# Attention's Strassen products on one Trainium2 core: two banks filled turn by turn in place of one after the other

## The reference

```python
memory_proj = jnp.einsum('bme,de->bmd', memory, W_mem)
scores = jnp.einsum('bnd,bmd->bnm', hidden_states, memory_proj) / jnp.sqrt(jnp.float32(D))
attn = jax.nn.softmax(scores, axis=-1)
memory_context = jnp.einsum('bnm,bmd->bnd', attn, memory_proj)
gate_input = jnp.concatenate([hidden_states, memory_context], axis=-1)
gate = jax.nn.sigmoid(jnp.einsum('bnf,df->bnd', gate_input, W_gate) + b_gate)
fused = hidden_states + gate * memory_context
return _rmsnorm(fused, norm_w)
```

## Time and profile before

| | us |
|---|---|
| median of 3 runs | 933.08 (931.79 to 933.41) |
| the profiled execution, its own time | 933.24 |
| its span in the trace | 931.5 |
| PE busy | 915.3 (98%), 4412 matmuls and 4412 weight loads |
| DVE busy | 738.0 (79%) |
| ACT busy | 415.3 (45%) |

### The profile page before, as it was taken

The page is one execution under the profiler, slowest core; times in us unless marked ns, Lnnn a source line. Parts: engine busy times, 40 slices in busy tenths (PEclk is TensorE's granted clock), DMA queues, the critical chain, the costliest instruction groups (busy, mean ns, idle before and its releaser), DMA issues.

```text
span 931.5 us, 11731 instructions
## 1 busy us (share of the span) xinstructions
PE 915.3 (98%) x4412; PEld 770.8 (83%) x4412; DVE 738.0 (79%) x969; ACT 415.3 (45%) x624; POOL 53.9 (6%) x74
## 2 busy tenths in 40 slices
PE   9999999999999999999999999999999999999996
PEld 8878888888888887788888888888888888888884
DVE  5975767776777669968786589888889888988887
ACT  5442222232222224554545456555555656555553
POOL 0000000000000000000000011001111111111002
PEclk9999999999999999999999999999999999999999
DMA  9433567546575646675648925555555544545542
GB/s 352 169 134 114 208 221 233 218 168 230 190 261 190 234 155 223 247 238 204 212 152 321 371 90 197 204 203 203 203 182 185 179 171 183 170 172 184 204 181 90
DMA packets 50408, 187.41 MB, mean 201 GB/s; under 512 B 5168, under 2 KB 7216, under 8 KB 43312
## 3 DMA queue, kind: packets, MB, share of 16 engines
q1 hardware_dynamic: 50064, 186.14, 56.2%
q10 hardware_dynamic: 288, 0.52, 0.2%
HBM read 130.02 MB, written 56.62 MB: 200 GB/s over the span
## 4 chain that ended last, share of the span: by engine, by line
PE 85%; DVE 7%; issue 4%; ACT 2%; DMA 1%; SPq 1%; POOL 0%; DVEq 0%; POOLq 0%; ACTq 0%
PE psum L1271 28%; PE psum L1273 28%; PE psum L1272 28%; DMA g_raw<-in_g 1%; DVE g_l L796 1%; ACT yh L536 1%; DVE yt_raw L949 1%; PE psum L1353 1%; DVE b_l L796 0%; DVE y L1006 0%; DVE wn_l L796 0%; DVE ws_l L796 0%; DVE z L907 0%; SPq L286 0%; DVE g_raw L824 0%
## 5 line engine op out<-in xcount | busy, mean ns | idle before, releaser
L1271 PE MATMUL psum<-g1h,xh 128*128 128x512 f32 x448 | 175.3, 391 | 2.3 <-DVE k_out L917 2.2
L1272 PE MATMUL psum<-g_l,xh 128*128 128x512 f32 x448 | 174.8, 390 | 0.0
L1271 PEld LDWEIGHTS psum<-g1h,xh 128*128 128x128 f32 x448 | 84.5, 189 | 21.0 <-issue 3.5
L1273 PE MATMUL psum<-g1h,xs_l 128*128 128x512 f32 x256 | 100.3, 392 | 0.0
L1272 PEld LDWEIGHTS psum<-g_l,xh 128*128 128x128 f32 x448 | 84.5, 189 | 17.5
L536 ACT ACTIVATE xh<-xs_raw 128x512 fp32r<-128x512 f32 x64 | 40.3, 632 | 121.6 <-PE psum L1273 121.6
L1172 DVE TENSOR_TENSOR zb<-psum,zb 128x512 f32<-128x512 f32 x112 | 76.8, 686 | 15.8 <-PE psum L1273 15.7
L907 DVE TENSOR_TENSOR z<-psum,bias 128x512 f32<-128x512 f32 x64 | 44.2, 690 | 39.7 <-PE psum L1273 39.7
L1273 PE MATMUL psum<-g1h,xsum_l 128*128 128x512 f32 x192 | 74.7, 389 | 0.0
L507 POOL TENSOR_TENSOR stat<-stat 128x1 f32<-128x1 f32 x30 | 19.7, 658 | 860.1 <-ACT zb L739 860.1
L536 ACT ACTIVATE xh<-xsum_raw 128x512 fp32r<-128x512 f32 x48 | 30.1, 629 | 80.8 <-PE psum L1273 75.8
(11 more groups left out here) (172 smaller groups left out, 2417.5 us busy)
## 6 DMA issues: line engine op xcount, KB each, us to landing
xs_raw<-in_xt SPq DMA_DIRECT2D x16, 1024.0 KB, 4.8
z_spill<-z SPq DMA_DIRECT2D x16, 1024.0 KB, 7.8
b_raw<-in_xt SPq DMA_DIRECT2D x32, 512.0 KB, 6.5
zb<-z_spill SPq DMA_DIRECT2D x16, 1024.0 KB, 6.9
xrow<-in_x SPq DMA_DIRECT2D x30, 512.0 KB, 6.6
out<-xrow SPq DMA_DIRECT2D x30, 512.0 KB, 3.7
y_spill<-y SPq DMA_DIRECT2D x32, 256.0 KB, 2.7
yt_raw<-y_spill SPq DMA_DIRECT2D x16, 512.0 KB, 3.6
```

The source lines that it names most:

```text
L1271: nc.tensor.matmul(tile, ah, mh, start=start, stop=False, skip_group_check=True)
L1272: nc.tensor.matmul(tile, ah, ml, start=False, stop=False, skip_group_check=True)
L1273: return nc.tensor.matmul(tile, al, mh, start=False, stop=stop, skip_group_check=True)
```

## The change

In `mem_gate` the waits for both halves are now issued ahead of all matmuls of a product, and then the 12 matmuls go mem, gate, mem, gate, with the same stationary slice for both of a pair: for each k (0, 1) and part (high-high, high-low, low-high) one matmul of mem and one of the gate. `mem_mm` is raised by the 11th matmul in place of the 6th, `gate_mm` by the 12th as before. Product 6 of batch 15 keeps the old form. So 111 of 112 products are changed. Number, shapes and operands of the matmuls are the same, and so is what each bank accumulates.

```diff
--- before.py
+++ after.py
@@ -1436,10 +1436,23 @@
                             pe.wait_ge(z_done, P7 * b)
                         elif i >= 2:
                             pe.wait_ge(z_done, P7 * b + {2: 1, 3: 2, 4: 3, 5: 4, 6: 5}[i])
+                    if final:
+                        for k in range(2):
+                            last = three(bank(bk), th[:, slot, k, :], tl[:, slot, k, :], wb_h[m][i][:, k, :],
+                                         wb_l[m][i][:, k, :], False, k == 1)
+                        last.then_inc((mem_mm, gate_mm)[m], 1)
+                if not final:
+
                     for k in range(2):
-                        last = three(bank(bk), th[:, slot, k, :], tl[:, slot, k, :], wb_h[m][i][:, k, :],
-                                     wb_l[m][i][:, k, :], k == 0 and i in (0, 1, 3), k == 1)
-                    last.then_inc((mem_mm, gate_mm)[m], 1)
+                        for part in range(3):
+                            for m in range(2):
+                                bk = 2 * m + (p if i in (0, 2, 4, 6) else 1 - p)
+                                last = nc.tensor.matmul(bank(bk), (tl if part == 2 else th)[:, slot, k, :],
+                                                        (wb_l if part == 1 else wb_h)[m][i][:, k, :],
+                                                        start=k == 0 and part == 0 and i in (0, 1, 3),
+                                                        stop=k == 1 and part == 2, skip_group_check=True)
+                                if k == 1 and part == 2:
+                                    last.then_inc((mem_mm, gate_mm)[m], 1)
```

## The result

| | before | changed |
|---|---|---|
| median of 12 runs, us | 933.04 (931.44 to 935.40) | 935.26 (933.66 to 936.33) |
| the profiled execution, its own time | 933.24 | 934.14 |
| its span | 931.5 | 932.4 |
| weight loads, matmuls | 4412, 4412 | 4412, 4412 |

The ratio is 1.0020, 95% interval 1.0011 to 1.0029: slower by 1.9 us (1.0 to 2.7), distinct from no difference, and right on the bound of 0.2% that the prediction set. The forecast was 935.0.

The account below looks back on a forecast made before the run. It took PE, busy 98% of the span, as the bound, with matmul rate unchanged. Rate 0, batch 1 0.2 and batch 15 1.74 sum to +1.9 us over the 933.08 median: 935.0, range 933.4 to 937.2.

Parts of the forecast that it names:

- bound of 0.2%: Whole kernel: a measurement can tell about 0.2% (1.9 us) from no change, 934.95; 50% slower, 45% same, 5% faster.
- Nothing idle on TensorE, rate unchanged: Attention's products: PE busy 25.33 of 25.33 us a batch; matmuls stay 0.227 us apart, sharing and alternating banks cost 0.
- price of 0.230 us a matmul: Upper bound on the rate: 0.230 us in place of 0.227 for 1332 matmuls would cost 4.4 us.
- Rival 3: Clock falls after batch 15's new 0.6 us stall: 1.7 us more, 936.7; chance 4%.
- Price of a late release: Attention's products: first matmul starts 0.15 us behind a late release, 0.08 more lost after; 0.23 ahead costs nothing.
- Batch 1, +0.2: Product 2 of batch 1 waits for z_out, starting 557.30 instead of 557.18, then loses 0.08 more: +0.2 us.
- Batch 15, product 3, +0.6: Product 3 of batch 15 waits for z_out(15, 1), held behind fuse(14, 1), and starts at 912.22: +0.6 us.
- Batch 15, `mem_add` 5, +1.13 and +1.74 in all: Batch 15's end: mem's signal 5 matmuls later delays mem_add 5 by 1.13; with PE's 0.60, +1.74 us.
- Batches 2 to 14, margin 0.59, cost 0: Product 2 there: z_out 0 ends 0.82 us ahead, 0.23 needed, so 0.59 remains and the moved wait costs 0.
- Rival 4: DVE sets each batch's pace at product 2's wait for z_out 0: 937.6; together with rate 0.230 (939), chance 9%.
- The nearest of ACT's copies: Copy of product 6 ends 1.32 us ahead of the next batch's product 1, so mem's later signal costs 0 there.
- Sum +1.9, 935.0: Whole kernel: 0 for the rate, 0.2 for batch 1, 1.74 for batch 15, +1.9 us, giving 935.0 us.

Follow-up runs that it names:

- e5: Changed kernel, but mem takes k = 0, 1 and the gate k = 1, 0, so no neighbours share a slice; stage 404.45 us against 404.48.
- e2: Batches 0 to 14 alternate, batch 15 as in the kernel before; 933.35 us median, ratio 0.9995 to the kernel before, stage +0.19 us.
- e7: Changed kernel plus an unread VectorE maximum over 1024 columns ahead of z_out 0 in batches 2 to 14; stage 411.20 us, +8.68 against the kernel before.
- e8: Kernel before plus an unread VectorE maximum over 1024 columns ahead of z_out 0 in batches 2 to 14; stage 404.32 us, +1.80.
- e9: Changed kernel; in batch 15 mem_add 1 and z_out 1 precede fuse(14, 1), ACT copies product 2 sooner; stage 403.94 us, +1.42 against the kernel before.
- e3: Kernel before with only product 3 of batch 15 alternating; stage 403.11 us, +0.59.
- e4: Kernel before with only product 5 of batch 15 alternating; stage 403.65 us, +1.13.
- e6: Changed kernel plus an unread VectorE maximum over 256 columns ahead of z_out 0 in batches 2 to 14; stage 404.42 us, +1.90 against the kernel before.
- e11: As e9, with fuse_quarter(1) also ahead of mem_add 5 on VectorE; 934.42 us median against 933.30 before, ratio 1.0014, stage +1.17.
- e12: Kernel before, with other PSUM banks for the gate's x part in the first two batches; 929.36 us median against 933.46, ratio 0.9957.
- e1: Kernel before with only batch 15 alternating (products 0 to 5); 935.05 us median against 933.29, ratio 1.0020, stage +1.74.
- e10: Kernel before with the two batch 15 reorders of e9; 933.26 us median against 933.30, ratio 0.9994, stage -0.01.

## Why the prediction was right, point by point

- **Nothing idle on TensorE, rate unchanged.** Right. A middle batch took 25.33 us before and after, 4412 weight loads stayed, and e5 shows that sharing has no worth. The price of 0.230 us a matmul, kept as an upper bound, was not seen in the batches of the middle. The Trainium skill, "TensorE: Matmul & The Clock Gate", section "Step-by-step: what each phase is for", says that weights can be loaded once for many matmuls. This program's trace has one load for each matmul, with pairs on one slice too, so the order of the matmuls alone does not give that use of it, and no run here shows what it would bring.
- **The clock.** Rival 3 did not occur: with banks changing at every matmul the granted clock of a middle batch was 1.00, and the wait of 0.5 us in batch 15 did not lower it: the clock stayed at 1.00 to 925.6, behind the last matmul (922.2). The Trainium skill's rule on cycling through PSUM banks, of the page "TensorE: Matmul & The Clock Gate", section "A second HAM failure mode: psum-queue depth-cycling", speaks of brief idling between groups. Here PE was busy 25.33 of 25.33 us, so the trace neither contradicts the rule nor shows it.
- **Price of a late release** (0.15 behind its end, 0.08 more behind that): the 0.15 came up in the changed kernel and in e2, e7, e8 and e9 each time (0.14 to 0.15). What a product took longer behind it was 0.06 (e7) to 0.12 us (product 3 of batch 15, before and changed). That 0.23 us ahead is needed is not shown: the nearest release that cost nothing ended 0.35 ahead.
- **Batch 1, +0.2.** Measured 0.22 (377.21 - 376.99), and 0.21 in e2 (377.20 - 376.99).
- **Batch 15, product 3, +0.6.** Product 3 started 3.39 us behind product 2, as worked out; e3 alone 0.59.
- **Batch 15, `mem_add` 5, +1.13 and +1.74 in all.** Measured 17.08 - 15.35 = 1.73; e4 alone 1.13; the piece behind it kept its length (10.19 us in both traces).
- **Batches 2 to 14, margin 0.59, cost 0.** Right, and e6 and e7 put the edge between 0.33 and 1.13 us of added DVE work. Rival 4's condition was not met. e7 shows its mechanism, at 0.51 us a batch for 1.13 of delay.
- **Margins that were passed over, without cost.** The nearest of ACT's copies was not 1.32 us ahead: the copy of batch 0's product 6 ended 0.47 ahead of batch 1's product 1 (551.11 and 551.58), and that of batch 1's product 2 1.01 ahead of product 4. In batch 15 `z_out` 0 ended 0.35 ahead of product 2. All three cost nothing in the changed kernel either (0.47, 1.22 and 0.35), so the 0 was right, but for these places it had not been worked out, and that it held was luck in part.
- **Sum +1.9, 935.0.** The stage gave +1.96, the medians 2.2, their ratio 1.9 us. The 0.3 between stage and medians lies within the interval and stays unexplained; the half-clock stretch, which a run has or has not, does not account for it, since within the cluster of runs around 933.0 and 935.3 the difference is 2.3 too. The mechanism and the size were forecast. On which side of 0.2% the ratio would fall was not, and the prediction said so.
- **What I had wrong** lies for the most part in the experiments: in e8 I weighed one margin against one delay and did not ask whether DVE has room for the added work in each batch, and in e9 and e11 I removed a stall without pricing the release, and in e11 the instruction, that was next in line.

## What to carry to other kernels

When two independent groups of matmuls are interleaved, all waits of both move to the first matmul, and all signals of both to the last ones: price each moved wait by the margin of its release, and each moved signal by what its reader leads to, batch by batch, because the first and last rounds have other lists around them than the middle. On an engine that is busy all the time, such an edit can only gain through the rate of its instructions, and two rows (distance of neighbours that share, and of neighbours that change banks) tell that before anything is run. Where an engine gets more work in every round, compare it with the time that this engine waits for the others in a round, not with the margin of one release: what it can't get back is added again in the next (e8). Where a stall is taken out, name the release that is late next, and look at places with a single long wait: e12's two lines were worth twice what this change cost.

## What the runs showed of the hardware that I had not expected

- The times of a kernel stand in clusters, and one wait makes them. In the traces the wait near 50 us, 1.5 to 3.4 us long, was followed by a stretch at granted clock 0.50 of 3.4 us (before, e1, e2, e3, e5 to e8), 6.8 us (e9), or none (changed, e4, e10, e11). The 21 runs of before beside e10 and e11 lie at 931.6 to 932.0 (4) and 933.0 to 933.9 (17). In e12, with 0.3 us of the wait left, its 6 runs lie within 0.6 us, and its trace has no such stretch.
- The length of the wait does not sort these traces (2.2 us with the stretch in before, 2.4 without it in e10). The start does: TensorE begins at 1.46 or 1.47 us in all of them, with 28 transposes 0.21 us apart. In the nine traces with the stretch their distance falls to 0.11, and the granted clock rises from half to full, at 4.5 to 6.4 us. In the four without it the clock rises at 7.2 to 7.5 us, and all or nearly all of the transposes are 0.21 apart. e12's clock rose at 4.4 us, as e9's did (4.5), and e9 had the longest stretch, so that e12 has none is not the luck of a late rise: it is the wait that is missing. Why the rise comes sooner or later, and how it bears on what the wait does to the clock, stays open.
- A short wait of TensorE does not appear among the waits; this is of the view, not of the chip. Starts 0.12 to 0.16 us late are not listed, one 0.45 us late is. The short ones show in the starts alone: 0.15 us from the end of the releasing instruction to the matmul, and 0.305 to 0.31 us to the next one in place of 0.227. The second sign is not enough by itself: product 5, behind the transposes, has 0.31 us there in every batch, with nothing late.
